# A two-layer network on one core: the stage that makes queries, keys and values of the second layer, with its rotary products read from PSUM and its head's scale moved to GpSimd

## What is computed

```python
qkv = jnp.einsum('bnh,hm->bnm', x, w_qkv)          # 2048 x 512 by 512 x 1536
q, k, v = jnp.split(qkv, 3, axis=-1)               # then 16 heads of 32 numbers each
q = rmsnorm(q, q_gamma)                            # x * rsqrt(mean(x^2) + eps) * gamma, per head
k = rmsnorm(k, k_gamma)
q = q * cos + rotate_half(q) * sin                 # rotary turn: halves of 16 numbers change places
k = k * cos + rotate_half(k) * sin
scores = jnp.einsum('bhqd,bhkd->bhqk', q, k) / np.sqrt(HD)   # causal, window 1024, softmax, times v
```

## Time and profile before

| | |
|---|---|
| median of three runs | 1680.03 us |
| profiled execution, its own time | 1680.31 us |
| its span (first to last instruction) | 1678.3 us |
| mean granted TensorE clock | 0.964 |
| busy, share of the span | PE 92%, DVE 61%, ACT 43%, POOL 28% |
| `stage_qkv`, first to last compute | 663.8 to 832.8 us |
| `stage_attend1` begins, SP asks for its first values | 839.1 us |
| first product with those values (L1928) | 862.5 us |

### The profile page before, as it was taken

The page is one execution under the profiler, slowest core; times in us unless marked ns, Lnnn a source line. Parts: engine busy times, 40 slices in busy tenths (PEclk is TensorE's granted clock), DMA queues, the critical chain, the costliest instruction groups (busy, mean ns, idle before and its releaser), DMA issues. The chain is left out here.

```text
span 1678.3 us, 23348 instructions
## 1 busy us (share of the span) xinstructions
PE 1551.0 (92%) x7008; PEld 1069.0 (64%) x7008; DVE 1022.2 (61%) x2739; ACT 721.1 (43%) x1218; POOL 478.1 (28%) x692
## 2 busy tenths in 40 slices
PE   5999999999999998799788999999999988899898
PEld 4877888887667776577554555555555535647484
DVE  5453666666566544888766776666668755575121
ACT  5533656656664323233224545555555541116010
POOL 0001777776431324322311212221221232130000
PEclk9999999999999999899859999999999999999899
DMA  4002222121002224376792404404413206514200
GB/s 170 1 1 82 100 73 103 69 103 51 25 26 96 94 82 137 102 189 172 204 300 80 110 5 111 114 18 99 110 35 83 62 18 203 202 37 201 100 1 12
DMA packets 96826, 158.75 MB, mean 95 GB/s; under 512 B 7956, under 2 KB 59220, under 8 KB 89176
## 3 DMA queue, kind: packets, MB, share of 16 engines
q1 hardware_dynamic: 92216, 147.28, 28.9%
q0 software_dynamic: 2208, 6.10, 1.4%
q10 hardware_dynamic: 2304, 4.20, 0.7%
HBM read 114.67 MB, written 42.87 MB: 94 GB/s over the span
## 5 line engine op out<-in xcount | busy, mean ns | idle before, releaser
L2010 ACT ACTIVATE l_pt<-banks 128x1024 f32<-128x1024 f32 (+3 forms) x288 | 218.5, 811 | 162.4 <-PE banks L1891 160.5
L2079 DVE CUSTOM_DVE_ANT_0 stage<-banks,l_edges 128x384 f32<-128x384 f32 (+3 forms) x384 | 201.6, 541 | 101.2 <-issue 100.1
L1928 PE MATMUL banks<-l_pt,l_v 128*64 128x512 f32 (+3 forms) x1152 | 231.4, 523 | 2.5 <-POOL l_pt L1985 2.4
L699 POOL TENSOR_TENSOR ex_hl<-ex_h,ex_hh 128x512 fp32r<-128x512 f32 x128 | 165.3, 1298 | 81.4 <-ACT ex_hh L667 81.2
L1984 POOL TENSOR_TENSOR l_turn<-l_before 128x2 f32<-128x2 f32 x192 | 39.8, 207 | 424.0 <-ACT l_pt L2010 414.6
L2082 DVE TENSOR_REDUCE l_mx<-banks 128x1 f32<-128x384 f32 (+1 forms) x208 | 113.1, 544 | 51.1 <-PE banks L1869 50.4
L732 DVE SCALAR_TENSOR_TENSOR ex_rw<-banks,ex_wb 128x512 f32<-128x512 f32 x128 | 88.3, 690 | 79.2 <-PE banks L75 79.1
L1928 PEld LDWEIGHTS banks<-l_pt,l_v 128*64 128x64 f32 x1152 | 70.6, 140 | 96.4 <-issue 72.8
L667 ACT ACTIVATE ex_hh<-ex_h 128x512 fp32r<-128x512 f32 x128 | 80.9, 632 | 103.7 <-DVE ex_h L740 101.8
L1869 PE MATMUL banks<-k,q 96*128 96x384 f32 (+3 forms) x296 | 94.2, 409 | 17.9 <-PEq L2716 7.6
L73 PE MATMUL banks<-ex_xlh,ex_wh 128*128 128x512 f32 x256 | 101.7, 397 | 2.0 <-DVE ex_rw L732 2.0
(11 more groups left out here) (409 smaller groups left out, 3444.0 us busy)
## 6 DMA issues: line engine op xcount, KB each, us to landing
ex_wb<-gates_by_expert SPq DMA_DIRECT2D x16, 1024.0 KB, 4.8
layer_v<-qkv_vs SPq DMA_DIRECT2D x16, 512.0 KB, 3.2
layer_qk<-qkv_yh SPq DMA_DIRECT2D x32, 256.0 KB, 3.7
layer_qk<-qkv_yl SPq DMA_DIRECT2D x32, 256.0 KB, 3.9
l_v<-layer_v SPq DMA_DIRECT2D x8, 1024.0 KB, 16.4
ex_ws<-ew_in SPq DMA_DIRECT2D x16, 384.0 KB, 5.0
l_q<-layer_qk SPq DMA_DIRECT2D x12, 512.0 KB, 7.8
l_k<-layer_qk SPq DMA_DIRECT2D x12, 512.0 KB, 13.7
```

Of the source, the lines that this page charges most:

```text
L699: pool.tensor_tensor(hl[:, k % RING, :], h[:, k % RING, :], raw(hh[:, k % RING, :]), ALU.subtract).then_inc(hl_done, 1)
L1928: last = pe.matmul(bank[h * 2 * HD:(h + 1) * 2 * HD, (qa - b * BT) * P:(qz + 1 - b * BT) * P], v[par][:, kt, h, :], pt[:, step_part(b, j), ...
L2010: act.activation(pt[:, step_part(b, j), :, 0:width], G.banks[:, 2 * slot:2 * slot + 2, 0:width], ACT.Exp, scale=scale).then_inc(p_done, 1)
L2079: dve.tensor_tensor_reduce(cutoff[:, n % 4, 0:width], G.ps[5 + n % MB][:, 0:width], masked, 1.0, NEG, ALU.add, ALU.max, mx[:, h, m, c:c + ...
```

## The change

In `stage_qkv`:

- VectorE multiplies the raw product, straight from PSUM, by the cosine table and by the sine table and adds the two (`turned`, three lines where L1598, L1609 and L1615 stood). The scale 1/root comes last, as GpSimd's only work per tile (`y`), two instructions. A head's scale is one number per token and head, so the order doesn't matter to the result. The banks of a product are free when `turned` is done.
- The tables are loaded first, on SP's queue, ahead of the value weights; the gammas come as one array in one transfer. GpSimd issues no transfer.
- The value product of a tile runs two tiles late instead of one. At the start the order is queries(2), transposes(0), keys(2), values(1), transposes(1), and the first value product takes the weights piece by piece. At the end values 14 and 15 stand between keys(15) and transposes(15).
- The stage no longer waits for its stores; their semaphores live on, and SP, GpSimd and VectorE wait for them at the start of `stage_attend1`. ScalarE issues the last two stores. A tile's values are stored after the heads of the next tile (but the last two, which go ahead of the last heads).
- GpSimd's write of ones into `G.k0` moves from the stage's end to its middle.

In `stage_attend1` VectorE makes a smaller mask first and fills `l_mrow` only before the fourth reduction, and GpSimd writes the ones into `l_k` only after six reductions.

```diff
@@ stage_qkv, SP @@
+            for k, n in enumerate(("cos32", "sin32")):
+                sp.dma_start(cs[k], I[n].rearrange("(t p) d -> p t d", p=P)).then_inc(tab_in, 16)
+            sp.dma_start(gam, I["gammas"].partition_broadcast(P)).then_inc(tab_in, 16)
             weights.load(sp, NC, None)
+            for t in range(NT):
+                if t == NT - 1:
+                    store_values(t - 1)
+                    store_values(t)
+                for k in range(2 if t < NT - 1 else 1):
+                    if k == 0:
+                        sp.wait_ge(hl_done, 2 * (t + 1) - (t == NT - 1))
+                    store_heads(sp, t, k)
+                if t in (0, 1):
+                    store_values(t)
+                if 3 <= t < NT - 1:
+                    store_values(t - 1)
                 if t % BT == 1 and t > BT:
                     first_pair(t // BT - 1)
-            for k in range(2):
-                sp.wait_ge(v_out[k], 16 * NT // 2)
-                sp.wait_ge(qk_out[k], 64 * NT // 2)
             sp.wait_ge(first_in, 96 * (NB - 1))
@@ TensorE @@
-            transposes(0)
-            for t in range(2, NT):
+            queries(2)
+            transposes(0)
+            keys(2)
+            values(1)
+            transposes(1)
+            for t in range(3, NT):
                 queries(t)
                 keys(t)
                 transposes(t - 1)
-                values(t - 1)
+                if t >= 4:
+                    values(t - 2)
+            values(NT - 2)
             values(NT - 1)
             transposes(NT - 1)
@@ ScalarE, the end @@
+            value(NT - 2)
             value(NT - 1)
             high(NT - 1)
+            act.wait_ge(hh_done, 2 * NT)
+            act.wait_ge(hl_done, 2 * NT)
+            store_heads(act, NT - 1, 1)
@@ GpSimd @@
+                pool.wait_ge(rs_done, t + 1)
                 for k in range(2):
...
+                    pool.tensor_tensor(y[:, k, :].rearrange("p (h d) -> p h d", h=H0),
+                                       t2[:, k, :].rearrange("p (h d) -> p h d", h=H0),
+                                       rs[:, t % 2, k, :].unsqueeze(2).to_broadcast([P, H0, HD]), ALU.mult).then_inc(y_done, 1)
+                if t == NT // 2:
+                    pool.wait_ge(y_done, 2 * (t + 1))
+                    pool.memset(raw(G.k0[3 * HD:3 * HD + 2, :, :]), 1.0).then_inc(ones_done, 1)
@@ VectorE @@
+            def turned(t, k):
+
+                dve.wait_ge(sq_done, 2 * t + k + 1)
+                wait(dve, y_done, 2 * (t - 1) + k + 1)
+                q4 = G.ps[2 * (t % 2) + k].rearrange("p (h d) -> p h d", h=H0)
...
+            for t in range(1, NT):
+                turned(t, 0)
+                means(t)
+                turned(t, 1)
+                inverses(t)
+                low(t - 1)
             low(NT - 1)
@@ stage_attend1 @@
+            for n in range(2):
+                dve.wait_ge(G.v_out[n], 16 * NT // 2)
+            dve.memset(edges[:, P:BANK], 0.0)
+            dve.memset(mx[:, :, :, :], NEG)
             dve.tensor_copy(edges[:, BANK:BANK + P], G.lower[:, :])
-            chain.done(dve.tensor_copy(edges[:, 0:P], G.upper[:, :]))
-            dve.memset(mx[:, :, :, :], NEG).then_inc(kones, 1)
+            dve.tensor_copy(edges[:, 0:P], G.upper[:, :]).then_inc(kones, 1)
...
+            pool.wait_ge(a_red, 2 * MB)
+            pool.memset(raw(k[1][K3:KM, :, :]), 1.0).then_inc(far_ones, 1)
```

More of the change, by code:

```diff
@@ L1430, in first_pair, with store_values @@
                                      ).then_inc(first_in, 16)
-            weights.load(sp, NC, None)
-            for t in range(NT):
-                rows = slice(t * P, (t + 1) * P)
+            def store_values(t):
                 sp.wait_ge(v_sb, t + 1)
@@ L1474, in keys @@
                 if t >= 2:
[L1475 removed]
+                    pe.wait_ge(sum_done, 2 * (t - 2) + 2)
                 if t == 0:
@@ L1485, in values @@
             def values(t):
+                wait(pe, v_sb, t - 1)
                 if t == 0:
-                    weights.ready(pe, 1)
-                wait(pe, v_sb, t - 1)
-                product(t, "v", 4 + t % 2).then_inc(v_mm, 1)
+                    for c in range(NC):
+                        pe.wait_ge(weights.w_lo, NC + c + 1)
+                        last = mm3(pe, G.ps[4], [(x(0, c), (w["v"][0][:, c * D:(c + 1) * D], w["v"][1][:, c * D:(c + 1) * D]))],
+                                   start=c == 0, stop=c == NC - 1)
+                    last.then_inc(v_mm, 1)
+                else:
+                    product(t, "v", 4 + t % 2).then_inc(v_mm, 1)
             keys(0)
@@ L1530, in value @@
                                ACT.Copy).then_inc(v_sb, 1)
-            weights.high(act)
+            weights.high(act, 0, NC)
             squares(0, 0)
+            weights.high(act, NC, NC + 2)
             squares(0, 1)
+            weights.high(act, NC + 2, NC + 3)
             root(0)
+            weights.high(act, NC + 3, 2 * NC)
+            squares(1, 0)
+            squares(1, 1)
             act.wait_ge(ones_done, 1)
-            for t in range(1, NT):
+            value(0)
+            root(1)
+            high(0)
+            squares(2, 0)
+            squares(2, 1)
+            value(1)
+            root(2)
+            high(1)
+            for t in range(3, NT):
                 squares(t, 0)
@@ L1577, in _ @@
             chain = Chain(dve, link)
-            weights.low(dve)
+            weights.low(dve, 0, NC + 2)
             def low(t):
@@ L1584, in low, with means @@
                                       raw(yh[:, t % 2, k, :, :]), ALU.subtract).then_inc(hl_done, 1)
-            for t in range(NT):
+            def means(t):
                 dve.wait_ge(sq_done, 2 * (t + 1))
@@ L1589, in _, with inverses @@
                 wait(dve, sd_done, t)
[L1590 to L1591 removed]
                 dve.tensor_scalar(ms[:, :, :], ms[:, :, :], 1.0 / HD, RMS_EPS, ALU.mult, ALU.add).then_inc(ms_done, 1)
[L1593 to L1594 removed]
+            def inverses(t):
                 dve.wait_ge(sd_done, t + 1)
[L1596 to L1600 removed]
@@ L1616, in _ @@
+            means(0)
+            weights.low(dve, NC + 2, NC + 3)
+            dve.wait_ge(tables, 2)
+            turned(0, 0)
+            weights.low(dve, NC + 3, 2 * NC)
+            inverses(0)
+            turned(0, 1)
+            for t in range(1, NT):
[4 more added lines that the diff above has]
+                low(t - 1)
             low(NT - 1)
@@ L1965, in _ @@
         def _(pool):
-            pool.memset(raw(k[1][K3:KM, :, :]), 1.0).then_inc(far_ones, 1)
-            pool.wait_ge(far_ones, 1)
+            for n in range(2):
+                pool.wait_ge(G.v_out[n], 16 * NT // 2)
             pool.memset(before[:, :], 1.0).then_inc(iota_done, 1)
```

109 lines of the change are left out of this document (46 added, 63 removed).

## The result

| | before | after |
|---|---|---|
| median | 1682.66 us (8 runs) | 1666.09 us (8 runs) |
| lowest to highest | 1674.94 to 1685.38 | 1661.85 to 1670.91 |
| ratio after/before | | 0.991, interval 0.990 to 0.993 |
| profiled execution, its span | 1680.31, 1678.3 | 1670.91, 1669.2 |

The change makes the kernel 14.8 us faster by the ratio (16.6 by the medians); 1662.5 (1653 to 1675) was predicted. The profiled execution of the kernel after is the slowest of its eight runs, so the end of its trace isn't used to judge the size. Each stretch is judged by distances inside it. The block of `stage_qkv`, its first compute, begins at 663.81 before and 664.66 after.

The account below looks back on a forecast made before the run. TensorE was taken to bound the middle of stage_qkv, with idle stretches at its ends. Head 7.5, middle 3.3, tail 5.0 and entry 2.0 sum to 17.8 us, so 1680.3 becomes 1662.5 us (1653 to 1675).

Parts of the forecast that it names:

- Head: Start of stage_qkv up to queries(3): tables loaded first and the new order save 7.5 us (4 to 10).
- Middle: Thirteen tiles of stage_qkv: transposes stop waiting for VectorE and GpSimd, 0.25 us a tile, 3.3 us (0 to 4.5).
- Half-head products: VectorE's sine products in stage_qkv, now read from PSUM: 0.41 us each, upper bound 0.8.
- Tail: From the last value product to the next stage: transposes(15) no longer wait, the stage ends earlier; 5.0 us (4 to 8).
- late value store: End of stage_qkv: ScalarE's last value copy waits for tile 13's store until 3 us after the last value product.
- Entry: Start of stage_attend1 up to its first reductions: smaller mask and later write of ones save 2.0 us (0.5 to 2.8).
- The stall of the one conversion: stage_attend1, after the negation of maxima: GpSimd's write of ones may hold VectorE's small conversion 1.6 us.
- Sum: Whole kernel: head, middle, tail and entry together save 17.8 us, and the attention stage carries the shift on.
- rival 1: Tables load slowly and the late value store costs more: gain only 5 to 12 us, about 1671 us; 17%.
- Rival 2: Attention stage's clock rises 6 to 10 us earlier: gain 24 to 30 us, 1653 us; 8%.
- Rival 3: GpSimd's scale is dear and closes a loop with TensorE: slower kernel, 1697 us at 5 us per scale; 4%.
- Rival 4: The later stage takes the gain back through transfers that moved less than the computation: 1679 us; 6%.

Follow-up runs that it names:

- e4: Kernel after, but tables and gammas are loaded on GpSimd's queue again and the value weights come first on SP's: 1673.43 us.
- e5: Kernel after, but VectorE splits the last quarter of the value weights before turned(0,0) instead of behind it: 1665.65 us.
- e12: Kernel after with the arithmetic of before in the qkv stage, and the last value-weight split before tile 0: 1675.91 us, ratio 0.997.
- e3: Kernel after, but GpSimd makes each scale three times over, with the same result: 1687.77 us.
- e1: Kernel after, but SP stores the values of tile 13 before the heads of tile 14: 1664.37 us, ratio 0.990.
- e7: Kernel after, but SyncE waits at the end of the qkv stage for all its stores, as before: 1670.94 us.
- e2: Kernel after, but GpSimd writes the ones into l_k after twelve reductions instead of six: 1661.65 us.
- e11: Kernel after, unchanged, run again beside other variants on the same chip: 1666.14 us, ratio 0.992.
- e6: Kernel after, but values run one tile behind, as before, with their copies and stores moved along: 1664.78 us.

## Why the prediction was right, point by point

- **Head**: forecast 7.5, measured 5.5 (35.73 to 30.22 from the block's start to queries(3)). The step that was mis-sized is VectorE's chain beside and behind the table products. The tables landed by 669.8, as forecast, but the gammas behind them at 671.9, not 670, and the table products took 5.9; e4 shows that this hardly matters. Two splits of the value weights took 3.48 us beside the table products, and the scaling of the means 0.90 instead of 0.18 beside GpSimd's write, where I had taken them as cheap. So the last split, put at 678.3, ended at 681.3 and the last quarter of values(0) waited for it until 681.34; queries(2) started at 682.8 and not 679. The clock then ran at half over them, 4.96 us instead of the 3.5 reckoned. Of the head's gain with e5's split about half is the new arithmetic: e12, with the old arithmetic, has queries(3) at 31.9, against 28.1 in e5 and 35.7 before.
- **Middle**: forecast 3.3, measured 5.1 (127.01 to 121.95). The mechanism was right, the size off. The term that was too small is what transposes lose inside, waiting for VectorE's second sum: I took 0.1. Before, 1.02 us pass from their start (753.04) to the values', in TensorE's timeline; now 0.79:

```profile
754.06 0.48 PE L73 MATMUL banks<-qkv_vh,xTh 128*128 128x512 f32 x1
```

So 0.23 a tile, and 9.55 - 9.15 = 0.4 a tile, times 13, is 5.2.
- **Half-head products**: 0.41 as taken. The Trainium skill (GPSIMD Engine Reference, section Key points) says that GpSimd contends with VectorE instructions that have two SBUF inputs. The trace agrees where GpSimd reads too: with both inputs in SBUF 0.409 to 1.516 in e12, and in e3 with one in PSUM 0.411 to 0.416 beside its scales. Beside a mere write of GpSimd it doesn't: a sum with both inputs in SBUF kept its 0.69 (last section). In the kernel after the half-heads were mostly alone, so there GpSimd's new place would by itself explain the 0.41.
- **Tail**: forecast 5.0, measured 3.3 (12.55 to 9.24). The late value store was foreseen; it came at E + 4.1 and not E + 3, though it was issued 0.8 us earlier than reckoned. The term that was too small is the landing, taken as 3.2 and measured as 4.9 (issued 815.92, landed 820.8). That isn't special to the tail. The 3.2 of the earlier trace rows belongs to an order in which a tile's values are stored ahead of its heads; the change stores them behind, and the source view of all 16 value stores (L1442) has

```profile
DMA to landing us min/median/max: 3.2/4.9/5.9
```

The one value store of before that stood behind four stores of heads (828.84) took 4.6 as well. Another 0.5 are ScalarE's two issues, 1.5 us (823.39 to 824.89) instead of 1.0. e1 puts the price of the late store at 2.2 us, e7 the gain of not waiting at 3.8.
- **Entry**: forecast 2.0. The first reduction came 3.35 us nearer to the stage's start (4.24 to 0.89), and 1.76 came back up to the first rows (7.15 to 8.91): 1.6 net. The stall of the one conversion, left open in the prediction, is real: 1.61 us, and e2 gets 1.4 back.
- **Sum**: 5.5 + 5.1 + 3.3 + 1.6 = 15.5 up to the first rows, and 14.8 in the total. The first product with the next stage's values comes 12.0 us behind the first rows both before (862.52) and after (847.89), so the shift is whole up to there. That it is carried on to the end is shown only to within the spread: from the first rows to the end took 827.8 us in the profiled execution of before, 833.3 in that of the kernel after and 829.8 in e11's of the same kernel. What makes this spread stays open.
- **Rivals**: rival 1's cause (slow tables) is excluded by their landing at 669.8 and by e4, its number (gain 5 to 12) by the result; while the tables came in (666 to 668), 2,793 packets under 512 bytes moved in 2 us, 1,400 per us and not 600. Half of the rival, the dearer store, was true, and the value weights did come late for VectorE. Rival 2 isn't seen: after the stage change the clock is back at full 15.5 us behind the first rows (851.4) and was so 16.6 us behind them before (867.0), 1 us and not 6 to 10. Rival 3 is excluded by 1.05 us a scale, and e3 shows that its loop exists. Rival 4 is excluded by the result and by the 12.0 us above.

Three terms were too high, by 4.1 us together, and one too low by 1.8; that the total fell so near is partly luck.

## What to carry to other kernels

In a stage bound by TensorE, look inside the operation that waits as well: a wait for the second half of its inputs shows in no idle column, only as a longer distance to the next operation. Where two engines share a chain per tile, take VectorE's operands from PSUM while GpSimd works (e3 shows this part by itself), and give GpSimd the last step. A store that is queued behind others holds the buffer of an engine two tiles later; find the oldest buffer that the last tile needs and put its store first. And when a change turns the order of a queue round, the landing times of the old order no longer hold.

## What the runs showed of the hardware

- What GpSimd does beside VectorE matters, not only what VectorE does. A conversion of only 8 columns took 1.61 us beside GpSimd's write of two partitions (e2: 0.18 alone), and in e3 the scaling of the means 1.91 instead of 0.18. Both ended with the write. What VectorE had started behind the held instruction ended no earlier, although it reads PSUM: in e3 a product of 512 columns took 1.81 and the half-heads behind it 1.22, all until 774.70. e3's VectorE and GpSimd:

```profile
772.79 1.91 DVE L1633 TENSOR_SCALAR qkv_ms<-qkv_ms 128x32 f32<-128x32 f32 x1
```

```profile
771.14 3.52 POOL L1615 MEMSET k<- 2x4096 f32 x1
```

VectorE's sum with two SBUF inputs of 512 columns kept its usual length beside the same kind of write, as VectorE's and GpSimd's timelines of the kernel after show:

```profile
752.17 0.69 DVE L1649 TENSOR_TENSOR qkv_t<-qkv_t 128x512 f32<-128x512 f32 x1
```

```profile
750.25 3.52 POOL L1609 MEMSET k<- 2x4096 f32 x1
```

Beside GpSimd products the same sum took 1.20 (e3), and each of two splits of the weights nearly 1.8 (3.48 for two), where one alone took 0.69 (e5).
- GpSimd's product with one number per head spread over 32 columns took 1.05 us; its product with 32 numbers repeated over the heads had taken 1.35.
- How long the same store of 512 KB takes to land goes with what is queued ahead of it: 3.2 us where it is issued ahead of the tile's heads (median of before), 4.9 behind four stores of heads (median of the kernel after, its middle included), 7.7 for the last value store of e6, behind another value store in a stretch with a DMA share of 1.04 and 309 GB/s.
